# Channel mixing issued from inside the merged loop's last steps, on one PSUM bank per product, in a 16-run recurrent kernel

## The reference

```
xc  = layernorm(x1) * ln2_w + ln2_b
sx2 = concatenate([state[:, 0:1] - xc[:, :1], xc[:, :-1] - xc[:, 1:]], axis=1)   # one position back, minus here
xk2 = xc + sx2 * ffn_maa_k
xr2 = xc + sx2 * ffn_maa_r
rr  = sigmoid(xr2 @ Wfr.T)
kk  = square(relu(xk2 @ Wfk.T))
return x1 + rr * (kk @ Wfv.T)
```

## Time and profile before

| | |
|---|---|
| median of 3 runs | 1304.67 us (1304.26 to 1307.09) |
| profiled execution, its own time | 1298.35 us |
| its span, first to last instruction | 1296.4 us |
| PE / PEld / DVE busy over the span | 1173.4 / 988.5 / 982.0 us |
| ACT / POOL busy over the span | 759.7 / 601.7 us |

### The profile page before, as it was taken

The page is one execution under the profiler, slowest core; times in us unless marked ns, Lnnn a source line. Parts: engine busy times, 40 slices in busy tenths (PEclk is TensorE's granted clock), DMA queues, the critical chain, the costliest instruction groups (busy, mean ns, idle before and its releaser), DMA issues. The chain is left out here.

```text
span 1296.4 us, 34790 instructions
## 1 busy us (share of the span) xinstructions
PE 1173.4 (91%) x13056; PEld 988.5 (76%) x13056; DVE 982.0 (76%) x1715; ACT 759.7 (59%) x1683; POOL 601.7 (46%) x520
## 2 busy tenths in 40 slices
PE   3799999999999996899999999999999997754998
PEld 3688888888888875687787778787778785542887
DVE  3777777676666762158999889999889999894787
ACT  2577777677777764566655566655566554343332
POOL 2677777777777760133443443443443442320111
PEclk9899999999999998999999999999999998886999
DMA  9200000011111100000000000000000000000011
GB/s 364 68 3 0 0 0 0 9 36 43 32 40 32 40 18 1 1 1 1 1 1 1 2 1 1 0 0 0 0 0 0 1 1 2 1 1 0 33 40 57
DMA packets 24792, 26.98 MB, mean 21 GB/s; under 512 B 2256, under 2 KB 19984, under 8 KB 24080
## 3 DMA queue, kind: packets, MB, share of 16 engines
q1 hardware_dynamic: 23424, 24.42, 5.5%
q10 hardware_dynamic: 1296, 1.58, 0.3%
HBM read 21.79 MB, written 4.19 MB: 20 GB/s over the span
## 5 line engine op out<-in xcount | busy, mean ns | idle before, releaser
L1364 DVE TENSOR_TENSOR_SCAN late_st<-late_wT,late_st 128x512 f32<-128x512 f32 x128 | 184.3, 1440 | 4.4
L805 POOL TENSOR_TENSOR late_xm<-late_mixed,late_xa 128x512 f32<-128x512 f32 x80 | 93.6, 1178 | 156.5 <-DVE late_mixed L1336 150.2
L262 POOL TENSOR_TENSOR att_z<-att_z,att_row_max 128x512 f32<-128x512 f32 x128 | 130.7, 1042 | 11.2 <-DVE att_row_max L580 8.5
L814 POOL TENSOR_TENSOR late_st<-late_st,late_rT 128x512 f32<-128x512 f32 x32 | 40.7, 1270 | 192.3 <-DVE late_st L1364 192.3
L1358 DVE TENSOR_TENSOR late_st<-psum,late_kT 128x504 f32<-128x504 f32 x128 | 86.6, 677 | 52.4 <-PE psum L990 51.1
L875 PE MATMUL psum<-w,late_hT 128*128 128x256 f32 x512 | 121.7, 382 | 1.9 <-ACT late_hT L1120 1.9
L866 PE MATMUL psum<-late_glnT,w 128*128 128x256 f32 x512 | 117.8, 384 | 2.2 <-ACT late_glnT L1110 2.2
L875 PEld LDWEIGHTS psum<-w,late_hT 128*128 128x128 f32 x512 | 94.9, 190 | 19.9 <-issue 5.5
L866 PEld LDWEIGHTS psum<-late_glnT,w 128*128 128x128 f32 x512 | 96.3, 193 | 15.6 <-ACT late_glnT L1110 2.9
L255 POOL TENSOR_TENSOR att_z<-att_z,cross_bias 128x512 f32<-128x512 f32 x64 | 80.2, 1274 | 59.4 <-DVE att_z L573 57.8
L255 POOL TENSOR_TENSOR att_z<-att_z,self_bias 128x512 f32<-128x512 f32 x64 | 80.2, 1274 | 50.9 <-DVE att_z L573 50.9
(11 more groups left out here) (167 smaller groups left out, 2833.2 us busy)
## 6 DMA issues: line engine op xcount, KB each, us to landing
att_encT<-in_enc SPq DMA_DIRECT2D x64, 128.0 KB, 2.5
out<-x SPq DMA_DIRECT2D x16, 256.0 KB, 2.0
x<-in_x SPq DMA_DIRECT2D x1, 2048.0 KB, 11.5
w<-in_w SPq DMA_DIRECT2D x2, 1024.0 KB, 21.8
x<-in_x SPq DMA_DIRECT2D x1, 1024.0 KB, 6.9
cross_mask<-in_cross_mask SPq DMA_DIRECT2D x1, 1024.0 KB, 15.3
x<-in_x SPq DMA_DIRECT2D x1, 768.0 KB, 4.9
w_qkv<-in_w_qkv ACTq DMA_DIRECT2D x1, 768.0 KB, 15.6
```

The source lines that it names most:

```text
L262: nc.gpsimd.tensor_tensor(zs, zs, peak.unsqueeze(2).to_broadcast([P, PAIRS, S]), ALU.subtract).then_inc(shifted, 1)
L805: nc.gpsimd.tensor_tensor(xm[:, m % 2, :, :].rearrange("p h (b t) -> p (h b) t", t=S), mixed[:, m % 2, :, :].rearrange("p h (b t) -> p (h ...
L1364: nc.vector.tensor_tensor_scan(states, wT[:, u, half, :, :, :].rearrange("p j b t -> p (j b t)"), states, 0.0, ALU.mult, ALU.add).then_inc ...
```

## The change

`norm5` and `channel_phase` are gone; their work is issued by `late_phase`, in the same block.

The two drain steps 16 and 17 are written out, with channel-mixing work put between their instructions on every engine. The norm is made in two batches (NORMS): runs 0 to 12 with `ch_variances(0)` and `ch_invert(0)` in step 14 and `ch_shifts(0)` in step 15, runs 13 to 15 with `ch_variances(1)`, `ch_invert(1)`, `ch_shifts(1)` in the drain. It uses Ln and Exp in place of the square root and the reciprocal. In step 15 ACT normalises runs 0 to 2, PE transposes runs 0 and 1, POOL makes their differences, DVE mixes run 0, and PE ends the step with keys and receptances of run 0.

Each product has one bank, so each waits for the reader of the run before. Normalising moves from DVE to ACT, the difference from DVE to POOL, the square from POOL to ACT, the first slot's copy from DVE to ACT. The sigmoid becomes 0.5 + 0.5 tanh(x / 2): ACT makes the tanh, and `ch_finish` does (t + 1) * value and then 0.5 * that + x. The mixed inputs lie in the MLP's hidden buffer and the squares and gates in the recurrence's repeated values, both free by then. SP's loop of stores is the same, in the merged block.

The core of the diff (the bodies of the PE helpers hold the same matmuls as before; the removed phase is left out):

```diff
+        hidden = hT[:, :, :].rearrange("p h t -> p (h t)")
+        ch_xk, ch_xr = (hidden[:, i * 2 * HALVES * RT:(i + 1) * 2 * HALVES * RT].rearrange("p (u h t) -> p u h t", u=2, h=HALVES)
+                        for i in range(2))
+        spare = v_rep[:, :, :, :].rearrange("p c j n -> p (c j n)")
+        ch_kk, ch_rr = (spare[:, i * 2 * HALVES * RT:(i + 1) * 2 * HALVES * RT].rearrange("p (u n) -> p u n", u=2)
+                        for i in range(2))
+        ch_tr, ch_key, ch_recept, ch_value = mlp, proj, v_banks[0], v_banks[1]
...
+        NORMS = ((0, (RUNS - 3) * CH), ((RUNS - 3) * CH, RUNS * CH))
...
-            for s in range(RUNS - 4, RUNS + 2):
+            for s in range(RUNS - 4, RUNS):
                 body(s, s % 2)
+
+        def channel_runs(eng, body):
+            for s in range(TAIL, TAIL + 2):
+                body(s, s % 2)
+            with eng.Fori(TAIL // 2 + 1, RUNS // 2 - 2) as i:
+                body(2 * i, 0)
+                body(2 * i + 1, 1)
+            for s in range(RUNS - 4, RUNS):
+                body(s, s % 2)
...
+                if s_is(s, RUNS - 1):
+                    ch_shift(0, 0)
+                    ch_shift(1, 1)
+
+            def ch_shift(r, u):
+                pool.wait_ge(ch_xc_ready, r + 1)
+                if later(r - 1):
+                    pool.wait_ge(ch_mixed_ready, r - 1)
+                nc.gpsimd.tensor_tensor(ch_sx[:, u, :, :, :].rearrange("p h b t -> p (h b) t"),
+                                        ch_xc[:, u, :, :, 0:S].rearrange("p h b t -> p (h b) t"),
+                                        ch_xc[:, u, :, :, 1:S + 1].rearrange("p h b t -> p (h b) t"),
+                                        ALU.subtract).then_inc(ch_sx_ready, 1)
+
+            def channel(s, u):
...
+            channel(0, 0)
+            scale(RUNS - 1)
+            channel(1, 1)
+            channel(2, 0)
+            channel(3, 1)
+            channel_runs(pool, channel)
...
+                    if s_is(s, RUNS - 1):
+                        if n == 4:
+                            ch_transpose(0, 0)
+                        if n == 5:
+                            ch_transpose(1, 1)
+                        if n == 7:
+                            transpose_on(RUNS - 2)
+                            ch_keys(0, 0)
...
+            def ch_transpose(r, u):
+                pe.wait_ge(ch_xn_ready, r + 1)
+                if not later(r):
+                    pe.wait_ge(mlp_x, RUNS)
+                else:
+                    pe.wait_ge(ch_xc_ready, r)
...
+            def ch_keys(r, u):
+                pe.wait_ge(ch_mixed_ready, r + 1)
+                if not later(r):
+                    pe.wait_ge(gate_done, RUNS)
+                else:
+                    pe.wait_ge(ch_relu_ready, r)
...
+            def ch_receptances(r, u):
+                if not later(r):
+                    pe.wait_ge(kv_ready, RUNS * GROUPS_R - 1)
+                else:
+                    pe.wait_ge(ch_rr_ready, r)
...
+            def ch_values(r, u):
+                pe.wait_ge(ch_kk_ready, r + 1)
+                if not later(r):
+                    pe.wait_ge(kv_ready, RUNS * GROUPS_R)
+                else:
+                    pe.wait_ge(ch_rv_ready, r)
...
+            def channel(s, u):
+                if there(s + 2):
+                    ch_transpose(s + 2, u)
+                if there(s + 1):
+                    ch_keys(s + 1, 1 - u)
+                ch_values(s, u)
+                if there(s + 1):
+                    ch_receptances(s + 1, 1 - u)
...
+            project_out(RUNS - 2)
+            sum_heads(RUNS - 1, 2)
+            sum_heads(RUNS - 1, 3)
+            ch_transpose(2, 0)
+            transpose_o(RUNS - 1)
+            ch_keys(1, 1)
+            ch_values(0, 0)
+            ch_receptances(1, 1)
+            channel(1, 1)
+            transpose_on(RUNS - 1)
+            channel(2, 0)
+            project_out(RUNS - 1)
+            channel(3, 1)
+            channel_runs(pe, channel)
...
+            def ch_invert(i):
+                part = slice(*NORMS[i])
+                act.wait_ge(norm_var, i + 1)
+                act.wait_ge(gxn_ready, RUNS)
+                nc.scalar.activation(core.norm_tmp[:, 0, part], core.norm_tmp[:, 2, part], ACT.Ln,
+                                     bias=core.eps[:, :]).then_inc(norm_logged, 1)
+                act.wait_ge(norm_logged, i + 1)
+                nc.scalar.activation(core.rstd[:, part], core.norm_tmp[:, 0, part], ACT.Exp, scale=-0.5).then_inc(norm_rstd, 1)
+
+            def ch_normalise(r, u):
+                act.wait_ge(norm_ready, norm_of(r))
+                if later(r - 1):
+                    act.wait_ge(ch_xnT_ready, r - 1)
+                for c in range(CH):
+                    t = r * CH + c
+                    last = nc.scalar.activation(ch_xn[:, u, c, :], core.x[:, ds(t, C)], ACT.Identity,
+                                                scale=core.rstd[:, ds(t, 1)], bias=core.neg_mean[:, ds(t, 1)])
+                last.then_inc(ch_xn_ready, 1)
+
+            def ch_copy_in(r, u):
+                act.wait_ge(ch_xnT_ready, r + 1)
+                if later(r - 1):
+                    act.wait_ge(ch_mixed_ready, r - 1)
+                for half in range(HALVES):
+                    nc.scalar.activation(ch_xc[:, u, half, :, 1:S + 1],
+                                         ch_tr[:, half * RT:(half + 1) * RT].rearrange("p (b t) -> p b t", t=S),
+                                         ACT.Identity, scale=col(core, "r_ln2_w", half), bias=col(core, "r_ln2_b", half))
+                nc.scalar.activation(ch_xc[:, u, :, :, 0], core.state_rows[:, 0, :, ds(r, RB)],
+                                     ACT.Copy).then_inc(ch_xc_ready, 1)
+
+            def ch_nonlinear(r, u):
+                act.wait_ge(ch_key_ready, r + 1)
+                if later(r):
+                    act.wait_ge(ch_kk_ready, r)
+                else:
+                    act.wait_ge(vj_ready, RUNS * GROUPS_R)
+                nc.scalar.activation(ch_relu[:, :], ch_key, ACT.Relu).then_inc(ch_relu_ready, 1)
+                act.wait_ge(ch_relu_ready, r + 1)
+                if later(r - 1):
+                    act.wait_ge(ch_value_ready, r - 1)
+                nc.scalar.activation(ch_kk[:, u, :], ch_relu[:, :], ACT.Square).then_inc(ch_kk_ready, 1)
+                act.wait_ge(ch_recept_ready, r + 1)
+                if later(r - 1):
+                    act.wait_ge(ch_out_ready, r - 1)
+                nc.scalar.activation(ch_rr[:, u, :], ch_recept, ACT.Tanh, scale=0.5).then_inc(ch_rr_ready, 1)
+
+            def channel(s, u):
+                if there(s + 2):
+                    ch_copy_in(s + 2, u)
+                if there(s + 3):
+                    ch_normalise(s + 3, 1 - u)
+                if there(s + 1):
+                    ch_nonlinear(s + 1, 1 - u)
...
+                if s_is(s, RUNS - 1):
+                    ch_normalise(0, 0)
+                    ch_normalise(1, 1)
+                    ch_copy_in(0, 0)
+                    ch_normalise(2, 0)
...
+                if s_is(s, RUNS - 2):
+                    ch_invert(0)
...
+                if s_is(s, RUNS - 1):
+                    ch_copy_in(1, 1)
...
+            copy_on(RUNS - 2)
+            ch_nonlinear(0, 0)
+            copy_o(RUNS - 1)
+            channel(0, 0)
+            square(RUNS - 1)
+            nc.scalar.preload_act_table_set("natural_log_exp_and_others")
+            invert_deviations(RUNS)
+            nc.scalar.preload_act_table_set("gelu_apprx_tanh_and_others")
+            channel(1, 1)
+            copy_on(RUNS - 1)
+            channel(2, 0)
+            channel(3, 1)
+            nc.scalar.preload_act_table_set("natural_log_exp_and_others")
+            ch_invert(1)
+            nc.scalar.preload_act_table_set("gelu_apprx_tanh_and_others")
+            channel_runs(act, channel)
...
+            def ch_variances(i):
+                part = slice(*NORMS[i])
+                stats = core.stats[:, :].rearrange("p (t s) -> p t s", s=6)
+                mean_even, m2_even, mean_odd, m2_odd = (stats[:, part, j] for j in (1, 2, 4, 5))
+                a, b, c = (core.norm_tmp[:, j, part] for j in range(3))
+                dve.wait_ge(stats_ready, NORMS[i][1])
...
+            def ch_shifts(i):
+                part = slice(*NORMS[i])
+                dve.wait_ge(norm_rstd, i + 1)
+                nc.vector.scalar_tensor_tensor(out=core.neg_mean[:, part], in0=core.neg_mean[:, part], scalar=-0.5,
+                                               in1=core.rstd[:, part], op0=ALU.mult, op1=ALU.mult).then_inc(norm_ready, 1)
...
+            def ch_mix(r, u):
+                dve.wait_ge(ch_sx_ready, r + 1)
+                if not later(r):
+                    dve.wait_ge(down_ready, RUNS)
+                if later(r - 1):
+                    dve.wait_ge(ch_key_ready, r - 1)
+                    dve.wait_ge(ch_recept_ready, r - 1)
```

(74 more changed lines are left out.)

219 lines of the change are left out of this document (41 added, 178 removed).

## The result

The changed kernel takes 1288.38 us (median of 6 runs) against 1304.26 of the kernel before (6 runs beside it). The ratio is 0.9879, 95% interval 0.9852 to 0.9906, which is 12.3 to 19.3 us less. Forecast were 1286.6 us and a gain of 18.1; measured are 15.9. The profiled execution's own time is 1284.37, its span 1282.1. Two of all the executions behind this text, one of e10_both_spare (1702.42) and one of the kernel before beside it (1971.61), were slow at a granted clock of 0.65 and 0.57 and count in no median or ratio.

A forecast was written before the change was run, and what follows sets the result against it. Bound by a drain chained through all engines, then PE-bound channel mixing. Keys(0) start 1170.3 + PE work 94.8 + waits 5.4 + low clock 3.5 = 1274.0, 18.1 earlier; median 1286.6 us, range 1280 to 1296.

The forecast's parts named there:

- The forecast case: Whole kernel: the forecast's own case, a gain of 13 to 24 us, likeliest 18.1; chance 0.75.
- Start of keys(0): First channel product on PE: starts at 1170.3 (1168.8 to 1171.7), 27.8 earlier than 1198.12.
- The low bound of 1168.8: Start of the first keys on PE: the earliest time by the bounds, against 1170.3 forecast.
- PE's waits: PE in the drain, behind run 15's head: 5.4 us together, from 1 to 10; none in the steady part.
- Low clock: First products after PE's idle gap: one and a half to two run at 1.2 GHz, costing 3.5 us, 0 to 7.
- PE work and period: PE from keys(0) on: 94.8 us of work in all; a steady period of 5.64 a run instead of 5.81.
- The sum: End of the last product: 1170.3 + 94.8 + 5.4 + 3.5 = 1274.0, against 1292.08; span 1278.3.
- The drain keeps its waits: Rival, in the drain: run 15's head blocks more, waits of 10 to 20 instead of 5.4; chance 0.13.
- The period grows: Rival, steady channel mixing: DVE and POOL slow each other, period 6.7, twelve runs eat 13 us; chance 0.03.
- Slower by the clock: Rival, drain and first runs: PE stays at the low level, 5.64 more each run, median 1317 with six; chance 0.05.
- No gain: Rival, ACT in channel mixing: tanh's table set lacks relu or square, so table loads in every run; chance 0.01.

The follow-up runs named there:

- e10_both_spare: e4_both with nine spare products of weights, results unused, in PE's gap before keys(0); 1277.01 us, ratio 0.9801 to the kernel before.
- run 14: Not a follow-up run: one of the runs the kernel itself works through, the one before the last; no time of its own as a kernel.
- e8_diff_dve: The changed kernel with the channel mixing's difference moved from POOL back to DVE; 1285.61 us, ratio 0.9874 to the kernel before.
- e3_head_aside: The changed kernel with finish(2) and run 5's mixes ahead of run 15's residual on DVE, second norm batch's ACT and shift work later; 1285.98 us, ratio 0.9849.
- run 15: Not a follow-up run: the last of the kernel's own runs, whose chain goes through all engines in the drain; no time of its own as a kernel.
- e7_warm: The changed kernel with 20 spare matmuls, results thrown away, in PE's gap before keys(0); 1287.95 us, ratio 0.9882 to the kernel before.
- e5_norm_act: The kernel before with only the channel mixing's normalising moved from DVE to ACT; 1304.72 us, ratio 0.9993.
- run 6: Not a follow-up run: one of the kernel's own runs in the channel mixing; from it on one run each 5.62 us and no PE wait.
- e2_earlier: The changed kernel with run 0's difference ahead of scale(14), its mixes ahead of group 6, keys(0) ahead of run 14's transposes; 1286.16 us, ratio 0.9840.
- e4_both: The changed kernel with the edits of e2_earlier and e3_head_aside together; 1279.42 us, ratio 0.9814 to the kernel before.
- e9_all_dve: e4_both with each run's difference moved from POOL to DVE, in front of its mixes; 1277.02 us, ratio 0.9806 to the kernel before.

## Why the prediction was right

The forecast case came, and the parts can be checked against the landmark, with the 3.3 taken off.

- **Start of keys(0).** Forecast 1170.3, measured 1173.93 - 3.29 = 1170.6. The norm batch delays the sum of squares of run 14 by 0.8 (forecast 0.7: it starts at 1166.23, at 1162.15 in the earlier trace rows, less 3.29). Scale(14) is 1.98 and the mixes 2.43 as taken (1.99, 2.5), the hand-overs too. The difference took 1.5, not 1.2: the prediction had DVE at the end of group 6 and then idle, but its read-out still ran beside the difference for 0.6, until 0.94 before the mixes. (The low bound of 1168.8 has the difference at 1.2; the least of its row, 1.04, gives 1168.6.)
- **PE's waits.** Forecast 5.4, the rows give 5.1 of idle time: values(1) 0.80 (0.7), keys(3) 0.89 (1.1), values(2) none (0.5), values(3) 1.93 (1.3), values(4) 1.27 (1.3), keys(6) 0.24. Counted from start to start, with the short gaps and slower first matmuls around each, they cost 6.7 (values(1) start 2.70 after keys(2), where a product takes 1.73, so 0.97; keys(3) 1.06, values(2) 0.37, values(3) 2.09, values(4) 1.43, keys(6) 0.40, and 0.40 in the products behind them). The term of the forecast counts like that, so it was 1.3 too small. Most of this is values(3): the forecast had the queue right, but not the meeting of DVE and POOL in it, without which the wait is 1.07 in e8_diff_dve, 1.24 from start to start. e3_head_aside shows for the last three that the cause is the one named: run 15's head in front of channel work.
- **Low clock.** Forecast 3.5, measured (3.58 - 1.73) + (2.27 - 1.73) = 2.4; e7_warm shows that it is the clock. The forecast took two whole products at the low level; the clock was back during the second. In e3_head_aside and e8_diff_dve the same two products cost 2.8 and 2.9, so the price varies by some half a us.
- **PE work and period.** 1278.08 - 1173.93 is 104.15; less 6.7 and 2.4 it is 95.0, forecast 94.8. The period is 5.62, forecast 5.64, and e5_norm_act shows that DVE's normalising had made it 5.81.
- **The sum.** keys(0) to the end was forecast as 103.7 and is 104.15. That it comes this near is in part luck: the waits, 1.3 too small, and the low clock, 1.1 too large, nearly cancel. The span is 3.8 above the forecast 1278.3, of which 3.3 lie ahead of the landmark, in work that the change doesn't touch. For the median, 15.9 of 18.1 were measured; the stretch gives 17.3, and the timed interval (12.3 to 19.3) holds both.
- **The rivals.** The drain keeps its waits: they exist, at 5.1, not 10 to 20. The period grows: no; DVE and POOL do slow each other, at the first mixes and before values(3), but from run 6 on no wait is left. Slower by the clock: the granted clock was 1.00 from 1180 on, but in e2_earlier it fell after one wait of 1.94, for 1.75 and not for several runs, so this rival had a real place and too large a price. No gain: no table load comes after 1215.47.

What stays open is why the same wait before values(3) cost clock in e2_earlier and not in the changed kernel or e7_warm; one execution of each is all that was profiled.

The best kernels are e4_both, e9_all_dve and e10_both_spare, 1277 to 1279 us. They can't be told from each other.

## What to carry to other kernels

Where a phase bound by one engine stands behind a drain bound by a chain through all of them, look at the bound engine's gaps in the drain: 15.6 of 17.3 us came from filling these, and 1.7 from a leaner phase. Once it overlaps, go through each in-order queue and ask of every instruction of the old chain who needs it and when: moving those that nobody needed soon behind the new work was worth another 3.5 us of stretch, which the timed runs show only together with the earlier start (e4_both). Price the low clock from start to start, and before buying it back see which engine sets the next start. Where work moves to POOL, look for the DVE instructions that will run beside it, the smallest too.

## What the runs showed of the hardware that was not expected

- The landmark lay between 1118.9 and 1129.2 in these twelve executions, though the code before it differs in none of them. In the two profiles compared above, the clock fell in the merged loop's first steps of one and not of the other. The spread of 10.3 is two thirds of this change's gain, so one execution's span is a poor measure of a few us, and a stretch from a common landmark a better one.
- The clock can fall behind a short wait and be back two products later: 0.50 from 1214 to 1216 after 1.94 us of idle PE in e2_earlier and 1.00 from 1218 on, but 1.00 throughout after 1.93 in the changed kernel and 1.94 in e7_warm. In e10_both_spare it fell after 2.25 of idle time, right behind PE's unbroken work from 1164.25 to 1174.0.
- A DVE instruction on 128x6 numbers took 1.03 in place of 0.16 because it started beside POOL's difference of 1.04, and a product of the drain waited 0.9 longer for it.
